# Re-timing VectorE's normalisation chain in the last three layers of a graph network, and converting the first count tiles earlier

## The reference, cut to what matters

```
for l in range(3):
    msg = h[src] + h_edge_attr
    agg = segment_sum(msg, dst, num_segments=n)
    out = agg + h
    z = layernorm(out @ W1[l].T + b1[l], g1[l], be1[l])
    z = gelu(z)
    z = layernorm(z @ W2[l].T + b2[l], g2[l], be2[l])
    h = gelu(z + h)
```

## Time and profile before

| | us |
|---|---|
| three runs: median (lowest to highest) | 4795.1 (4792.8 to 4796.32) |
| the profiled execution's own time | 4790.99 |
| its span | 4789.2 |
| PE busy in the span | 4136.8 (86%) |
| DVE busy | 2971.1 (62%) |
| ACT busy | 1933.8 (40%) |
| POOL busy | 1971.2 (41%) |

### The profile page before, as it was taken

How to read it: one execution, slowest core, us unless ns; L and a number is a source line. 1 busy time by engine, 2 the same in 40 slices (tenths; PEclk the granted TensorE clock), 3 DMA queues, 4 the chain that set the end, 5 groups by cost and what they waited for, 6 DMA issues and landing times.

```text
span 4789.2 us, 100505 instructions
## 1 busy us (share of the span) xinstructions
PE 4136.8 (86%) x35231; PEld 3732.0 (78%) x35231; DVE 2971.1 (62%) x8078; ACT 1933.8 (40%) x4188; POOL 1971.2 (41%) x2199
## 2 busy tenths in 40 slices
PE   1599999999976788888888888888888998998997
PEld 1499999999965677777878778778777777777776
DVE  7799999999933344444444444444445667777676
ACT  1565565565531222222222222222214665666664
POOL 5511111111037777777777777777770000000000
PEclk9799999999989899999999999999999999999999
DMA  5444444444455567667667667767677776776875
GB/s 119 173 205 205 201 201 201 201 211 211 209 164 138 149 196 214 203 198 210 201 199 213 198 202 210 201 202 212 201 196 256 230 232 202 233 230 205 257 236 152
DMA packets 793921, 967.67 MB, mean 202 GB/s; under 512 B 124439, under 2 KB 674055, under 8 KB 781143
## 3 DMA queue, kind: packets, MB, share of 16 engines
q1 hardware_dynamic: 623488, 764.12, 47.4%
q0 software_dynamic: 60048, 125.37, 10.4%
q10 hardware_dynamic: 110151, 75.61, 6.2%
HBM read 707.25 MB, written 257.60 MB: 201 GB/s over the span
## 4 chain that ended last, share of the span: by engine, by line
PE 35%; POOL 35%; issue 15%; DVE 11%; DMA 3%; ACT 1%; POOLq 0%; ACTq 0%; DVEq 0%
POOL ACC L1047 33%; PE ps L1573 9%; PE ps L1942 7%; PE ps L1943 6%; PE ps L1557 4%; PE ps L1559 4%; DMA ACC<-table,BIG 2%; DVE T L2219 2%; DVE BIG L2219 2%; DVE COUNTS L2640 2%; PE ps L1858 1%; POOL ACC L971 1%; DVE ST L2682 1%; PE ps L1960 1%; PE ps L1978 1%
## 5 line engine op out<-in xcount | busy, mean ns | idle before, releaser
L1047 POOL DMA_INDIRECT ACC<-table,BIG x1715 | 1680.5, 980 | 626.2 <-issue 513.7
L1843 PE MATMUL ps<-BIG 128*128 128x257 f32 x3430 | 860.1, 394 | 146.5 <-ACT BIG L1248 145.9
L2462 DVE TENSOR_TENSOR BIG<-ps,ACC 128x512 f32<-128x512 f32 (+1 forms) x441 | 297.9, 676 | 1096.9 <-DMA ACC<-table,BIG 905.2
L1843 PEld LDWEIGHTS ps<-BIG 128*128 128x128 f32 x3430 | 635.3, 196 | 248.0 <-ACT BIG L1248 169.9
L1248 ACT ACTIVATE BIG<-BIG 128x512 f32<-128x512 f32 (+1 forms) x441 | 273.7, 621 | 1321.4 <-DVE BIG L2462 1309.8
L1573 PE MATMUL ps<-H,ACC 128*128 128x128 f32 x4802 | 690.4, 285 | 0.0
L1464 ACT ACTIVATE COUNTS<-X 128x512 fp32r<-128x512 bf16 (+1 forms) x1092 | 599.3, 598 | 147.4 <-PE ps L1943 141.1
L1573 PEld LDWEIGHTS ps<-H,ACC 128*128 128x128 f32 x4802 | 588.2, 192 | 0.2 <-ACT ACC L1189 0.2
L1189 ACT ACTIVATE BIG<-ps 128x392 bf16<-128x392 f32 x784 | 390.1, 498 | 468.2 <-PE ps L1559 468.2
L1942 PE MATMUL ps<-COUNTS,H_BIG 128*128 128x512 f32 (+1 forms) x1274 | 511.7, 402 | 57.9 <-DVE COUNTS L2640 38.1
L1943 PE MATMUL ps<-COUNTS,H_BIG 128*128 128x512 f32 (+1 forms) x1274 | 488.8, 384 | 0.0
(11 more groups left out here) (290 smaller groups left out, 7594.1 us busy)
## 6 DMA issues: line engine op xcount, KB each, us to landing
X<-count_mat SPq DMA_DIRECT2D x360, 512.0 KB, 4.8
weight_mat<-ACC SPq DMA_DIRECT2D x49, 3136.0 KB, 9.2
BIG<-in_edge_attr SPq DMA_DIRECT2D x392, 256.0 KB
count_mat<-BIG SPq DMA_DIRECT2D x49, 1568.0 KB, 12.8
REL_WT<-weight_mat SPq DMA_DIRECT2D x275, 256.0 KB
BIG<-rel_tab ACTq DMA_DIRECT2D x392, 128.0 KB
BIG<-weight_mat SPq DMA_DIRECT2D x176, 256.0 KB
X<-count_mat SPq DMA_DIRECT2D x108, 384.0 KB, 3.5
```

What stands on the lines that cost most here:

```text
L1047: pool.indirect_dma_start(GR[:, q * QUAD + u, :], None, tables[1], bass.IndirectOffsetOnAxis(ap=STEP_IDX[:, b % 3, r * QUAD + u:r * QUAD + ...
L1843: mm = pe.matmul(PS[4 + par][:, 0:HIW], DR[:, q * QUAD + u, :], HB[:, q * QUAD + u, :], start=(r == 0 and u == 0), stop=(r == QB - 1 and u ...
L2462: dve.tensor_tensor(HB[:, steps, 0:F], PS[n % 2][:, 0:size * F].rearrange("p (u f) -> p u f", f=F), GR[:, own, :], ALU.add).then_inc(rows_ ...
```

## The change

It does four things. In the z half of the chain it moves the statistics, the moments, the three root steps and the norm to later offsets and, with the roots, one step to a gap between two of DVE's conversions; all that follows is moved by four offsets (turned 20 to 24, z_gelu 23 to 27, y 25 to 29). In the y half it replaces norm, scale and addition (four, one and one instructions for a wide group) by `y_center`, (y - mean) x g2 per block, placed ahead of the second root step, and a `y_add` that multiplies by the root and adds h per block (four and four). The last steps move from 43, 45, 46 and 48 to 45, 47, 48 and 50. And the first seven conversions move from `dense_layers` into `final_chunks`, at its chunks 10, 11 and 12.

```diff
+EARLY_ITEMS = {C1 - 3: (0, 1), C1 - 2: (2, 3), C1 - 1: (4, 5, 6)}
-LAG_OF = {"sum_turned": 4, "z": 5, "z_bias": 9, "z_stats": 10, "z_moments": 12, "z_guess": 14, "z_root1": 15, "z_root2": 16, "z_root3": 17, "z_norm": 18,
-          "z_turned": 20, "z_gelu": 23, "y": 25, "y_bias": 29, "y_stats": 31, "y_moments": 33, "y_guess": 34, "y_root1": 35, "y_root2": 36,
-          "y_root3": 37, "y_norm": 39, "y_scale": 41, "y_add": 43, "out": 45, "high": 46, "low": 48}
+LAG_OF = {"sum_turned": 4, "z": 5, "z_bias": 9, "z_stats": 11, "z_moments": 13, "z_guess": 14, "z_root1": 16, "z_root2": 18, "z_root3": 20, "z_norm": 22,
+          "z_turned": 24, "z_gelu": 27, "y": 29, "y_bias": 33, "y_stats": 35, "y_moments": 37, "y_guess": 38, "y_root1": 39, "y_center": 40, "y_root2": 41,
+          "y_root3": 43, "y_add": 45, "out": 47, "high": 48, "low": 50}
...
 ACT and DVE, final_chunks
+            def early_counts(t):
+                if t == min(EARLY_ITEMS):
+                    act.wait_ge(onehot_ready, QN)
+                    act.wait_ge(group_summed, GROUPS0 + len(GROUPS_OF))
+                for i in EARLY_ITEMS.get(t, ()):
+                    if i % CSLOTS in CSLOTS_OF_ACT:
+                        converted(i)
...
                     slot(t, 1, high_part)
+                    early_counts(t)
...
 ACT and DVE, dense_layers
-                    if pos < len(ITEMS) and pos % CSLOTS in CSLOTS_OF_ACT:
+                    if CSLOTS <= pos < len(ITEMS) and pos % CSLOTS in CSLOTS_OF_ACT:
                         converted(pos)
...
 DVE
-            def y_scale(g):
+            def y_center(g):
                 l, nb, own = of_sb(g)
-                stepped("y_norm", g)
-                step("y_scale", g, dve.tensor_tensor(SB_ZY[:, 0:nb, :], SB_ZY[:, 0:nb, :], over_nodes(L_G2[l], nb), ALU.mult))
+                stepped("y_moments", g)
+                for j in range(nb):
+                    ins = dve.scalar_tensor_tensor(SB_ZY[:, j, :], SB_ZY[:, j, :], MV[:, 4 + j, 0:1], L_G2[l], ALU.subtract, ALU.mult)
+                step("y_center", g, ins)
 
             def y_add(g):
                 l, nb, own = of_sb(g)
-                stepped("y_scale", g)
+                stepped("y_center", g)
                 stepped("shift", g)
-                dve.tensor_tensor(H[:, own, :], SB_ZY[:, 0:nb, :], H[:, own, :], ALU.add).then_inc(yn_ready, 1)
+                stepped("y_root3", g)
+                for j in range(nb):
+                    b = own.start + j
+                    ins = dve.scalar_tensor_tensor(H[:, b, :], SB_ZY[:, j, :], rstd[:, 4 + j:5 + j], H[:, b, :], ALU.mult, ALU.add)
+                ins.then_inc(yn_ready, 1)
```

More of the change, by code:

```diff
@@ L1374, in block_support, with converted @@
                 act.activation(T1[:, b, :], PS[2][:, 0:P], ACT.Copy).then_inc(node_free, 1)
+            def converted(i):
+                act.wait_ge(raw_in[ITEMS[i][3] % RAWS], RAW_IN0[ITEMS[i][3] % RAWS] + 16 * (ITEMS[i][3] // RAWS + 1))
+                if i >= CSLOTS:
+                    act.wait_ge(counts_used, i - CSLOTS + 1)
+                act.activation(slot_counts(i), raw_counts(i), ACT.Copy).then_inc(act_converted, 1)
+            def early_counts(t):
[5 more added lines that the diff above has]
+                        converted(i)
             def final_chunks():
@@ L1457, in general_layers @@
                     staggered(act, ((1, turned_sum), (3, gelu_z), (2, std_z), (4, std_y), (4, layer_out)))
[L1459 to L1464, removed]
             def sum_turned(g):
@@ L1492, in dense_layers @@
             def dense_layers():
-                act.wait_ge(onehot_ready, QN)
-                act.wait_ge(group_summed, GROUPS0 + len(GROUPS_OF))
                 for pos in range(LAYER_END):
@@ L2528, in block_scale, with converted, early_counts @@
                 dve.scalar_tensor_tensor(nmr[:, own], MV[:, b, 0:1], -1.0, rstd[:, own], ALU.mult, ALU.mult).then_inc(xn_norm, 1)
+            def converted(i):
+                dve.wait_ge(raw_in[ITEMS[i][3] % RAWS], RAW_IN0[ITEMS[i][3] % RAWS] + 16 * (ITEMS[i][3] // RAWS + 1))
+                if i >= CSLOTS:
+                    dve.wait_ge(counts_used, i - CSLOTS + 1)
+                dve.tensor_copy(slot_counts(i), raw_counts(i)).then_inc(dve_converted, 1)
+            def early_counts(t):
+                if t == min(EARLY_ITEMS):
+                    dve.wait_ge(group_summed, GROUPS0 + len(GROUPS_OF))
+                for i in EARLY_ITEMS.get(t, ()):
+                    if i % CSLOTS not in CSLOTS_OF_ACT:
+                        converted(i)
             def final_chunks():
@@ L2633, in stages @@
                 staggered(dve, ((0, out_sum), (2, stats_z), (4, stats_y), *(((0, middle),) if middle is not None else ()), (4, shift_h), (2, norm_z), (4, norm_y)), behind)
[L2635 to L2640, removed]
             step_of = {}
@@ L2707, in root_step, with z_norm @@
                 step(f"{name}_root{n}", g, dve.scalar_tensor_tensor(rstd[:, cols], rcnt[:, cols], 1.5, rstd[:, cols], ALU.add, ALU.mult))
-            def sb_norm(g, name, k):
+            def z_norm(g):
                 l, nb, own = of_sb(g)
-                stepped(name + "_root3", g)
+                stepped("z_root3", g)
                 for j in range(nb):
-                    ins = dve.tensor_scalar(SB_ZY[:, j, :], SB_ZY[:, j, :], MV[:, k + j, 0:1], rstd[:, k + j:k + j + 1], ALU.subtract, ALU.mult)
-                return ins
-            def y_scale(g):
+                    ins = dve.tensor_scalar(SB_ZY[:, j, :], SB_ZY[:, j, :], MV[:, j, 0:1], rstd[:, j:j + 1], ALU.subtract, ALU.mult)
+                ins.then_inc(zn_ready, 1)
+            def y_center(g):
                 l, nb, own = of_sb(g)
-                stepped("y_norm", g)
-                step("y_scale", g, dve.tensor_tensor(SB_ZY[:, 0:nb, :], SB_ZY[:, 0:nb, :], over_nodes(L_G2[l], nb), ALU.mult))
+                stepped("y_moments", g)
+                for j in range(nb):
+                    ins = dve.scalar_tensor_tensor(SB_ZY[:, j, :], SB_ZY[:, j, :], MV[:, 4 + j, 0:1], L_G2[l], ALU.subtract, ALU.mult)
+                step("y_center", g, ins)
             def y_add(g):
                 l, nb, own = of_sb(g)
-                stepped("y_scale", g)
+                stepped("y_center", g)
                 stepped("shift", g)
-                dve.tensor_tensor(H[:, own, :], SB_ZY[:, 0:nb, :], H[:, own, :], ALU.add).then_inc(yn_ready, 1)
+                stepped("y_root3", g)
[3 more added lines that the diff above has]
+                ins.then_inc(yn_ready, 1)
             def low_part(g):
@@ L2733, in dense_layers @@
             def dense_layers():
-                dve.wait_ge(group_summed, GROUPS0 + len(GROUPS_OF))
                 for pos in range(LAYER_END):
-                    if pos < len(ITEMS) and pos % CSLOTS not in CSLOTS_OF_ACT:
+                    if CSLOTS <= pos < len(ITEMS) and pos % CSLOTS not in CSLOTS_OF_ACT:
                         converted(pos)
@@ L2751, in dense_layers @@
                     for g in behind(pos, "z_norm"):
-                        sb_norm(g, "z", 0).then_inc(zn_ready, 1)
+                        z_norm(g)
                     for g in behind(pos, "y_bias"):
@@ L2763, in dense_layers @@
                             root_step(g, "y", 4, n)
[L2764 to L2767, removed]
+                    for g in behind(pos, "y_center"):
+                        y_center(g)
                     for g in behind(pos, "y_add"):
```

## The result

The changed kernel takes 4743.9 us (median of four runs, 4739.2 to 4748.5) against 4793.95 for the kernel before beside it: 0.9897 of its time, interval 0.988 to 0.9914, about 50 us faster. A second set gave 4746.3 (0.9907, 0.9891 to 0.9922). The profiled execution took 4744.73 us, span 4742.9, so the spans differ by 46.3 us where the sum had 38.6.

A forecast was written before the change was run, and what follows sets the result against it. PE was taken to bound the layers, busy 977 of 1043 us. Terms 18.2 + 8.1 + 4.8 + 4.5 + 2.5 + 0.5 = 38.6, say 39, off the profiled 4791.0 gave 4752, median 4756; range 4732 to 4780.

The forecast's parts named there:

- z half: DVE's late tiles at offsets 17 and 19 of wide chains: both PE stops go, 1.4 us in each of 21 groups.
- The second stop: PE's wait for ACT's tile behind the last gelu: grows 0.52 us in 14 groups, 0.56 new in the last layer's seven.
- Narrow and mixed groups: Six narrow chains gain 1.35 us each, 8.1; three wide chains beside narrow items 1.6 each, 4.8; narrow y halves nothing.
- Start: PE's first items: early tiles gain 2.5 us, 3.7 if the clock held, 0 if PE's own branch took the whole wait.
- The tail: Last chain, running alone: a norm's pass fused away and the centring filling waits gain 0.5 us.
- A: Rival, y half: small instructions don't overlap, 0.96 us more per wide y half, 27 us lost, 4783; chance 0.10.
- B: Rival, y half: instructions at 0.58 us, as while POOL copied, 78 us lost and 39 won, 4834; chance 0.04.
- C: Rival, last gelu: the second stop takes 0.9 us back per group, 4775, chance 0.10; stronger form, no measurable gain, 0.06.
- E: Rival: the second stop stays as it is, 11 us more, and narrow y halves give 8, 4737; chance 0.15.
- D: Rival: transfers become the bound, late pieces taking half of the gain, 4775; chance 0.05.

The follow-up runs named there:

- the z half alone: The kernel before with only the z half's new offsets, y half unfused and moved by 4 offsets: 4763.1 us, 0.9934 of the kernel before.
- the early tiles alone: The kernel before with only the first seven conversions moved into the final chunks: 4792.2 us, 0.9997 of the kernel before.
- the y half alone: The kernel before with only the fused y half (centring at 36, addition at 41), out, high and low unmoved: 4781.3 us, 0.9975.
- The fillers: The changed kernel with 8, 12, 10 and 5 extra PE products at items 1, 3, 6 and 7, into a bank nothing reads: 4744.9 us.
- the second kernel that has them: The changed kernel with own sums at offset 27, z gelu at 28, out and high at 50, low at 52, plus the extra PE products: 4701.1 us.
- three such moves: The changed kernel with DVE's own sums at offset 27, z gelu at 28, out and high at 50, low at 52: 4701.9 us, 0.9813.

## Why the prediction was right, point by point

**z half.** Right in mechanism and size. In the wide groups 0.37 + 0.11 and 0.92 us, by the medians, went at offsets 17 and 19, as 1.4 said, and some 0.1 more at the turn.

**The second stop: right mechanism, two terms too large.** It was to grow by 0.93 - 0.41 = 0.52 us. It grew by about 0.35, since the y half lost 0.62 us (8.07 to 7.45) and not 0.41. Half of the missing 0.2 is a wait between dependent instructions: in the kernel before the third root step starts 0.19 us behind the second one's last instruction with nothing between (4207.77 to 4207.96), and now a conversion lies there. The prediction named such a wait and left it out, but it is not the centring that fills it. Another 0.06 is the spacing, since the centring and the addition take 1.05 and 1.13 us where 1.08 and 1.16 were counted; the rest is in differences of some 0.01 us a row. In the last layer 0.56 us were to come up new, and 0.17 did. There the prediction took off 0.54 for the missing high part, from 4212.46 to 4213.00 in the earlier trace rows. But the high part waits for the gelu's end, and what falls away is 4212.46 - 4211.80 = 0.66. 14 x 0.17 + 7 x 0.39 = 5.1 us, of the 7.7 by which the sum was short.

**Narrow and mixed groups.** 8.3 against 8.1, by two errors that cancel, which is luck: the z half alone gave 1.08 each, not 1.35, and the y half, counted as nothing, gave 0.3. Of the mixed three one gave 1.5, as reckoned (1.6), the others 2.6: in the trace of before PE's granted clock was 0.50 for 2.5 us behind the stop at offset 19 in those two (3985.0 to 3987.5, and 0.52 from 4699.0 to 4701.6), and 1.00 in the third. One of the two, and the group that kept its clock:

```profile
3985.00:3987.50 2.50, 2.50 (x10) 2.50 (x10) 0.60 (x2) 2.34 (x5) 0.00 (x0) 0.50 0.59 161
4341.00:4343.50 2.50, 2.27 (x15) 1.95 (x15) 0.80 (x2) 2.49 (x6) 0.00 (x0) 1.00 0.62 166
```

With the early tiles alone the stop at 19 was as long and the clock 1.00 in all three, 2.1 us less; with the y half alone it fell in the group that had kept it (0.51 from 4331.0 to 4333.5) and in neither of the others. So 2 us of the 46.3 are that, and not the z half; what decides in which group the clock falls stays open.

**Start: the mis-sized term.** 2.5 us predicted, 1.1 by the medians. The sum charged 1.2 us for the lower clock. PE stood before items 2, 4, 7 and 8, and in the first trace the lower level lasted to 3700. Counted from the first statistics, item 8, the first tile that DVE converts behind its branch, came 2.9 us earlier than in the kernel before and item 24 only 1.0, so some 2.0 us went to the lower level. The 1.2 rests on a misreading as well: only the first two products start 0.57 us apart (3694.87 and 3695.44 in the trace of before), the next two 0.42, and an item takes 0.85 at that level. The fillers show that the clock is the cause: with the clock held it is 1.1 + 2.5 = 3.6 us, or 2.8 by the second kernel that has them; the prediction gave 3.7 for that case. Item 0 came at 3680.9, not 3685, since PE waited only 1.56 us for its branch, and item 7 at 3693.65, not 3696. The tail gave 0.3, not 0.5.

**The rivals.** A and B fall (that DVE slows beside POOL, as B had it, shows in the 32nd group, but not at these instructions; see the last section). The four centrings start 4187.85, 4188.11, 4188.37 and 4188.64: 0.26 apart, where A needed 0.39 and B 0.44. The rule of the Trainium skill ("VectorE: DVE Perf Modes", section on the TRN2 errata) that many small tiles pay the fixed latency many times does not decide here: eight instructions of 128 columns replace four of 128 and two of 512, and the y half is 7.45 us against 7.82 unfused at nearly the same offsets. C's mechanism is real (the z half alone gave 13.8 us back), but the fusion paid for it. E, no growth of the second stop, fails by the 0.35 us by which that stop grew, though the time lies between its 4737 and the forecast. D falls: the faster kernel drew 234 GB/s at a share of 0.79, and what the conversions waited for was PE, 156.4 of 161.9 us on ACT and 130.6 of 132.0 on DVE.

## What to carry to other kernels

In queues of fixed order, count what stands between two conversions of one engine against the work that the consumer does meanwhile; the excess is the stop. An instruction that waits long (here ACT's gelu, for DVE) goes behind the tiles that are due before its result is, not ahead of them: three such moves, of one to fifteen offsets, gave as much as the whole change, 44.2 us. When a consumer is to start early, look at what its gaps do to its clock.

## What the runs showed of the hardware

The spacing of DVE's 128-column instructions went by the operands beside the main one, in the four forms that ran here: they start 0.20 us apart with one that is not a constant (a column, or a tensor: the split centring), 0.26 with two (two columns in the norm, a column and a tensor in the fused steps), by the medians of the start-to-start times.

A narrow tile of 384 columns takes DVE longer to convert than a wide one of 512: 0.55 us against 0.43, and 0.46 us from start to start where conversions stand in a row. PE needs 0.35 us for a narrow item and 0.465 for a wide one, so narrow groups have the least room on DVE. Why the smaller tile takes longer, no run here tests.

One group (the 32nd) keeps a stop of 2 to 5 us in every trace, and in most of them PE's granted clock is low for a while behind it (0.66 from 4559 to 4564 us in the changed kernel). There POOL makes five additions in a row, which the reference's x + h needs. POOL, and DVE beside it, in the changed kernel:

```profile
4552.41 6.59 POOL L1108 TENSOR_TENSOR ACC<-ACC,H 128x512 f32<-128x512 f32 x5 [872.03 <-DMA ACC<-x_tab]
```

```profile
4555.34 1.25 DVE L2711 TENSOR_SCALAR nmr<-MV 128x4 f32<-128x4 f32 x1
4556.62 1.19 DVE L2713 TENSOR_SCALAR rstd<-nmr 128x4 int32<-128x4 int32 x1
4557.84 1.18 DVE L2719 TENSOR_TENSOR rcnt<-rstd,nmr 128x4 f32<-128x4 f32 x1
4559.05 0.16 DVE L2721 SCALAR_TENSOR_TENSOR rcnt<-rcnt,rstd 128x4 f32<-128x4 f32 x1
```

Instructions of 0.16 us last 1.2 while POOL adds, one for each of the last three additions, two conversions ahead of them last 1.44 and 1.23 us instead of 0.43, and the y half takes 12.44 us instead of 7.46. The Trainium skill ("SBUF — State Buffer", section "Who interferes with whom") says that a DVE instruction with two SBUF inputs, or one in a mode that uses both ports, and a GpSimd instruction that reads SBUF take turns, whole instruction by whole instruction; the rows agree, since the third instruction ends at 4559.02 us and the last addition at 4559.00, though no row tells whether the first two, which have one input, ran in such a mode. That stop was in the kernel before as well, and no run here took it away.
